# One kernel, five engines: all instruction orders and the PSUM banks of a Mamba-style layer written anew

## The chip, the cores and the metric

The kernel runs on one NeuronCore of a Trainium2 chip. The core has five engines with instruction streams of their own: TensorE (PE, matrix products), VectorE (DVE), ScalarE (ACT, which also evaluates tables of functions), GpSimd (POOL) and SyncE (SP), which here issues every DMA. They meet only at semaphores. The metric is the device time of one launch in microseconds; smaller is better.

## The reference

The input x is 8 x 1024 tokens of 256 channels, float32. All weights are float32 too. What is computed, cut to its core:

```python
# L0_attn, on u = layernorm(x); x = x + result
zxbcdt = u @ W_in.T                      # z0, x0 (512 each), xBC (512+16+16), dt (8 heads)
dt  = softplus(dt + dt_bias);  A = -exp(A_log)
xBC = silu(causal_conv4(xBC) + conv_b)   # depthwise, 4 taps
def step(h, x_t, B_t, C_t, dt_t):        # state 8 heads x 64 x 16, over 1024 tokens
    h   = exp(dt_t * A) * h + dt_t * x_t * B_t
    y_t = h @ C_t + D_param * x_t
y = layernorm(y) * ln_gamma + ln_beta
y = sigmoid(y @ W_gate.T + b_gate) * y
out = concat([silu(z0) * x0, y]) @ W_out.T
# L0_ffn, on layernorm(x); x = x + result
h = gelu(x @ absmean(W_fc))              # absmean: weights rounded to -1, 0, 1
h = layernorm(h) * ln_w + ln_b
out = h @ absmean(W_proj)
```

## The kernel before

**Tiling.** The 8192 tokens are 16 blocks of 512 (two blocks are one sequence), each of 4 chunks of 128 tokens, and the scan works on sub-chunks of 64. A float32 product is made of three float16 products of high and low halves (`products`, line 413), a product with ternary weights of two. Activations are turned by DMA transposes (`xnT`, `yhl`, `x3T`, `hT`) or on TensorE with an identity.

**Steps.** Each engine has a dictionary STEPS from a letter to a small function, and one string that says in which order its steps are issued: PE_ORDER, ACT_ORDER, DVE_ORDER, POOL_ORDER, SP_ORDER (lines 32 to 160). A word is a letter and a block number in hex; on PE the digits behind it are the PSUM banks (0 to 7) that the step writes. The n-th word with the same letter and block is part n of that step. The order of the words is the order of the instructions, and nothing else sets it. Several blocks are in flight at once: between the first convolution of a block and its last projection lie some 350 us, five blocks' worth.

**PE steps**, roughly in the order of one block: `c` convolution inputs (128x512 x6, line 413, and the small one of B and C at lines 483 to 485), `u` and `m` to `q` the decays (`q` line 581), `x` turns x (line 519), `g` the Gram product of B and C (line 555, it reads the tile `crep`), `e`, `b`, `s` small ones, `t` chunk states (line 568), `r` the part of y carried by the states (line 594), `w` the chunk's own part (line 613), `y` turns y (line 622), `G` gate (128x512 x12), `z` and `v` the skip branch (128x512 x6 each), `o` the output product (`wout`, 24 of 128x256), `f` the FFN's first product (line 673, 128x512 x4, two per chunk), `p` its second (line 685, 128x256 x16). `X`, `B`, `O`, `C`, `R` happen once, at the start.

**Waits.** Before a step writes a bank, `take` waits until the engine that last read it is done; other waits are for the operands. Each engine waits in its own order, so a step that waits holds up all that stands behind it. On DVE, `4` (function dt_last, lines 1112 to 1121) is a chain of six small instructions, each of which waits for the one before; `S` moves the state on eight times, `E` multiplies exponentials by the masked Gram matrix (line 1199), `v` (line 1236) and `c` (line 1081) read banks that PE then reuses. On POOL, `l` and `k` make the low halves of `cat` and `caty` (lines 1395, 1391), `n` adds the halves of y (line 1386), `q` and `V` are powers (line 1309). On ACT, exp and ln are in one table set, gelu in another, silu in a third; tanh is in the last two. `load` (line 183) issues ACT_TABLE_LOAD when the function wanted is not in the set that is there, so the order of ACT's steps sets how many loads there are. `E` on ACT (line 853) is the exponential, `F` (line 734) the sum of absolute weights, `g` gelu (line 914), `t` tanh.

**SP** issues DMAs in its order: `h` (xnT, line 1471, high half then low half, and then the load of x), `d` writes C to memory (line 1480), `c` spreads it over the partitions as `crep` (line 1487), `n` turns y (line 1515), `j` turns h (line 1525), `X`, `6`, `r`, `p` the others. A DMA whose data isn't ready holds up all behind it.

```python
def spread_c(i, n):
    sp.wait_ge(ce, i)
    sp.wait_ge(g_mm, i)
    sp.wait_ge(c_out, 32 * (i + 1))
    eng.dma_start(crep[:, :], c_rows[i % 2].unsqueeze(0).broadcast_to([8, 16, T])).then_inc(rep, 16)
```

Of the kernel before, what the change touches and what calls it, by code (L numbers as in the profile page):

```python
# [22 lines left out]
for _n, _w in (("alog", 8), ("dcol", 4), ("lng", 4), ("lnb", 4), ("bg", 4), ("cw", 20), ("cb", 5),  # L23
# [9 lines left out]
    "X00 X01 c02 c03 z04 c05 c06 u07 c00 B01 v02 z03 c17 m05 x01 s06 c10 x04 g035 x01 u14 c17 b06 x00 c13 e05 c14 "  # L33
    "q010 t026 v05 O07 q031 r00263 v01 z04 s15 m17 w0 w0 w0 w0 c24 y00 c27 x12 y06 y03 y01 z05 u24 x10 v02 z16 "
    "g104 c23 x10 z14 b15 e17 v11 x10 c22 c26 q175 G00 G03 t102 C01 G03 G06 r14302 q175 s27 m25 w1 v17 w1 w1 w1 "
    "x26 c31 c35 g247 x23 y10 o02 y11 x24 o07 y10 c36 u33 y11 z12 b23 o07 z10 C04 e21 o05 c34 x21 v17 R03 c31 G15 "
    "v16 G13 q220 z24 t275 q216 G13 G12 f00 r21576 w2 f03 f02 w2 w2 m30 f03 w2 f00 c42 s31 x35 f03 y27 x36 y20 "
    "o15 y24 c42 v27 z26 u43 x35 f07 f00 o11 v22 y27 g335 c44 b30 o11 e33 o15 x30 v27 c43 z21 p00 z26 c42 G25 "
    "q341 G23 t376 G25 v22 G20 z33 q325 p00 f16 v37 r33412 w3 f15 m46 w3 w3 f16 w3 f10 f15 c53 x47 s46 f14 y31 "
    "y30 p02 p07 c55 x43 z32 y31 o27 x44 g430 f16 u55 e41 o23 f10 b46 y37 c55 v34 o20 x43 o26 c57 c51 z30 p13 v32 "  # L40
    "z34 G36 q450 t472 G33 G34 v36 s53 q427 p15 m50 z41 G33 f22 r47654 w4 f23 w4 w4 f20 w4 f22 f23 c60 f27 y46 "
    "x55 v44 y42 p13 p17 y45 c61 u60 z46 x53 g572 o34 f23 x56 y40 c67 e52 f25 b56 o33 v41 o32 x54 o30 c66 p23 c65 "
    "z42 v44 t510 m67 z43 G46 G42 v40 q514 s63 G46 G45 q521 p24 f30 r53214 w5 z56 f37 w5 v55 w5 f36 w5 f30 f35 "
    "c77 x63 f32 y56 p21 y54 p20 c73 y55 x62 z51 o46 u77 e60 c72 x64 y55 o43 g617 b60 f34 v51 f37 o46 x65 o43 c70 "
    "c74 z51 p37 z56 v55 t632 G50 G51 q672 m73 z60 v56 s75 G54 G51 q606 p34 f41 v64 r67320 w6 f46 w6 w6 f41 w6 "
    "f44 f46 x71 c87 y63 p32 f44 y60 p36 x74 c81 y67 z62 e75 u86 o53 x74 y66 v60 b71 f45 g742 o57 c84 o52 f43 x71 "
    "c86 o57 z65 p40 c82 z63 v61 G67 t746 G65 m80 q727 v61 q734 s86 G65 p42 G67 r73461 f55 w7 f50 w7 z72 w7 f57 "
    "w7 f55 c90 f53 x87 y74 p46 f55 y71 c93 p47 y75 v70 z72 x84 e86 u97 o61 x80 b84 o62 y77 g853 f50 c96 v75 o63 "
    "f57 x81 o64 c92 z73 p51 c95 t807 z74 G76 v73 G74 m90 v77 q821 G76 q834 s95 p52 G71 z83 r84560 f67 w8 f62 w8 "
    "w8 f61 w8 f67 f62 ca4 x91 p55 y87 f66 ca0 y82 y86 p51 x97 z84 ua5 o71 b97 v85 e93 f62 x90 g964 o75 y83 v86 "  # L50
    "ca4 f60 o71 ca7 x92 o75 ca3 z81 p60 t962 G85 z84 v87 sa1 G85 ma2 q960 G87 q945 v81 p66 G83 f70 r94516 w9 f77 "
    "w9 w9 f73 w9 f72 f70 cb7 p64 xa3 y95 f71 y92 z96 p60 cb1 v97 y95 ub4 xa3 z96 cb0 ba2 f73 xa7 ea6 y95 o84 o81 "
    "v96 f77 xa4 o85 o82 ga31 cb6 z97 p75 cb3 ta14 G92 G90 mb7 z96 v92 qa14 G95 v90 qa62 p71 G94 f83 ra6201 wa "
    "f85 sb7 wa wa f84 wa p73 f85 f86 cc4 ya2 za0 f85 ya1 xb6 eb7 p73 cc4 ya2 va6 xb5 za3 uc0 o91 xb5 bb0 f82 o93 "
# [1545 lines left out]
```

## Time and profile before

| | |
|---|---|
| median of 3 runs | 1121.73 us (1119.06 to 1123.7) |
| the profiled execution | 1125.57 us |
| its span, first to last instruction | 1123.8 us |
| busy: PE, DVE, ACT, POOL | 1041.4, 981.4, 901.2, 500.2 us |
| mean granted clock of TensorE | 0.973 of full speed |
| ACT_TABLE_LOAD | 129, 165.5 us |

The busy time of PE is a union of overlapping matmuls whose ends are modelled, so the distance between starts says more than the length of one. A row of a timeline merges equal instructions that follow each other. Two of TensorE's clock levels are seen, 1.2 GHz (0.5 of the granted clock) and 2.4 GHz (1.0).

### The profile page before, as it was taken

What the parts mean: (1) busy time and instruction counts of PE and PEld (TensorE: products, weight loads), DVE (VectorE), ACT (ScalarE), POOL (GpSimd) and SP (SyncE); (2) the same over time, 40 slices, a digit from 0 to 9 for tenths busy, and PEclk for the clock granted to TensorE, in tenths of its full rate; (3) what the DMA queues carried; (4) which work ended last, traced back from release to release, by engine and by line L of the source; (5) the groups of instructions that cost most, each with busy time, mean ns of one, the idle gap of its engine ahead of it and who ended that gap; (6) DMA issues with size and microseconds to landing.
All of it is one profiled execution on the core that took longest, in us unless ns stands there. A gap on an engine that the chain in (4) does not pass through costs nothing. (4 is left out here: it accounts for less than half of the span.)

```text
span 1123.8 us, 29390 instructions
## 1 busy us (share of the span) xinstructions
PE 1041.4 (93%) x11470; PEld 661.2 (59%) x11470; DVE 981.4 (87%) x1992; ACT 901.2 (80%) x1593; POOL 500.2 (45%) x590
## 2 busy tenths in 40 slices
PE   5678899999999999999789999989999999999996
PEld 3343656565575756657456575755657565666674
DVE  6899999999989898998977999898999989777765
ACT  5768489878789888987767888988989986877875
POOL 2254562535345543452533435444554534554542
PEclk9889899999999999999998999999999999999998
DMA  8324233555553644455443465533544364263656
GB/s 270 73 58 59 67 61 67 88 98 93 97 109 66 132 74 99 95 88 114 91 76 73 87 114 92 104 64 77 116 92 109 64 110 77 58 124 56 125 118 146
DMA packets 303659, 106.20 MB, mean 94 GB/s; under 512 B 271904, under 2 KB 299808, under 8 KB 303520
## 3 DMA queue, kind: packets, MB, share of 16 engines
q1 hardware_dynamic: 303520, 104.31, 48.1%
q8 instruction: 91, 1.49, 0.5%
q14 instruction: 48, 0.39, 0.1%
HBM read 28.38 MB, written 8.91 MB: 33 GB/s over the span
## 5 line engine op out<-in xcount | busy, mean ns | idle before, releaser
L413 PE MATMUL bank<-xnT,win 128*128 128x512 f16 x1152 | 281.5, 389 | 4.1 <-DVE x L1242 1.9
L413 PEld LDWEIGHTS bank<-xnT,win 128*128 128x128 f16 x1152 | 111.6, 100 | 123.7 <-issue 11.5
L413 PE MATMUL bank<-yhl,wg 128*128 128x512 f16 x768 | 177.1, 383 | 7.7 <-DMA yhl<-ynh 3.0
L183 ACT ACT_TABLE_LOAD x129 | 165.5, 1283 | 2.3
L1395 POOL TENSOR_TENSOR cat<-sz,cat 128x512 f16<-128x512 f32 x64 | 84.0, 1313 | 176.8 <-ACT cat L902 176.7
L1391 POOL TENSOR_TENSOR caty<-tg,caty 128x512 f16<-128x512 f32 x64 | 88.3, 1384 | 132.2 <-ACT caty L890 132.2
L1081 DVE SCALAR_TENSOR_TENSOR cv<-bank,cws,cv 128x511 f32<-128x511 f32 (+2 forms) x192 | 142.8, 746 | 4.5
L685 PE MATMUL bank<-wpj,hT 128*128 128x256 f16 x1024 | 124.0, 276 | 7.4 <-DMA hT<-hb 7.2
L413 PEld LDWEIGHTS bank<-yhl,wg 128*128 128x128 f16 x768 | 73.5, 98 | 97.1 <-issue 9.5
L673 PE MATMUL bank<-wfc,x3T 128*128 128x512 f16 x512 | 129.4, 383 | 0.1
L685 PEld LDWEIGHTS bank<-wpj,hT 128*128 128x128 f16 x1024 | 99.7, 99 | 29.3 <-issue 10.7
L1309 POOL TENSOR_TENSOR rsy<-rsy,mhalf 128x1 f32<-128x1 f32 x64 | 43.6, 681 | 144.2 <-DVE rsy L1218 144.2
L914 ACT ACTIVATE h<-bank,rs 128x512 f32<-128x512 f32 x128 | 87.0, 681 | 25.0 <-PE bank L673 22.0
L413 PE MATMUL bank<-wout,cat 128*128 128x256 f16 x768 | 96.9, 277 | 1.8 <-POOL caty L1391 0.9
L413 PE MATMUL bank<-wout,caty 128*128 128x256 f16 x768 | 95.7, 275 | 0.0
L1256 DVE SCALAR_TENSOR_TENSOR h<-h,hmu,lnwb 128x1024 f32<-128x1024 f32 x64 | 89.5, 1398 | 6.1 <-ACT hsq L930 6.1
L1386 POOL TENSOR_TENSOR yT<-yhl 128x512 f32<-128x512 f16 x64 | 79.1, 1247 | 26.3 <-DMA yhl<-ynh 26.3
L1278 DVE TENSOR_TENSOR hb<-h,hb 128x1024 f16<-128x1024 f32 x64 | 82.3, 1286 | 7.6 <-ACT hb L947 6.0
L413 PEld LDWEIGHTS bank<-wout,cat 128*128 128x128 f16 x768 | 75.6, 99 | 18.0 <-ACT h L914 1.3
L863 ACT ACTIVATE tg<-bank,nmy,rsy 128x512 f32<-128x512 f32 x64 | 49.5, 774 | 40.6 <-POOL nmy L1381 32.9
L413 PEld LDWEIGHTS bank<-wout,caty 128*128 128x128 f16 x768 | 75.9, 99 | 9.4
L947 ACT ACTIVATE hb<-h 128x1024 f16<-128x1024 f32 x64 | 67.2, 1049 | 14.4 <-DVE h L1256 13.5
(167 smaller groups left out, 2099.4 us busy)
## 6 DMA issues: line engine op xcount, KB each, us to landing
x<-in_x SPq DMA_DIRECT2D x31, 512.0 KB, 4.8
out_y<-x SPq DMA_DIRECT2D x15, 512.0 KB, 3.3
crep<-c_rows SPq DMA_DIRECT2D x16, 256.0 KB
hT<-hb SPq DMA_TRANSPOSE x128, 3.2
caty<-in_wg SPq DMA_DIRECT2D x1, 1024.0 KB, 7.3
x<-in_wout SPq DMA_DIRECT2D x1, 1024.0 KB, 9.7
hT<-in_wfc SPq DMA_DIRECT2D x1, 1024.0 KB, 11.7
hb<-in_wpj SPq DMA_DIRECT2D x1, 1024.0 KB, 13.6
```

Of the source, the lines that this page charges most:

```text
L183: self.eng.preload_act_table_set(self.table)
L413: m = eng.matmul(b, lhs(p, k), rhs(q, k), start=(n == 0), stop=(n == len(seq) - 1))
L673: m = eng.matmul(b[:, :], x3T[:, p, c, k, :], wfc[:, k, half * T:(half + 1) * T], start=(k == 0 and p == 0), stop=(k == 1 and p == 1))
L685: m = eng.matmul(b[:, 0:DM], hT[:, buf, p, k, :], wpj[:, k, :], start=(k == 0 and p == 0), stop=(k == 7 and p == 1))
L914: eng.activation(h[:, at % 3, half * T:(half + 1) * T], b[:, :], ACT.Gelu, scale=rs3[:, c:c + 1], accum_out=hsum[:, c, half:half + 1]).the ...
L947: eng.activation(halves[h_halves(i, c)][:, 0, :], h[:, at % 3, :], ACT.Copy).then_inc(hn_hi, 1)
L1081: op = eng.scalar_tensor_tensor(cs[:, j, 3 - k:T], b[:, 0:T - 3 + k], cws[:, j, k:k + 1], cs[:, j, 3 - k:T], ALU.mult, ALU.add)
L1256: eng.scalar_tensor_tensor(h[:, at % 3, :], h[:, at % 3, :], hmu[:, c:c + 1], lnwb[:, :], ALU.subtract, ALU.mult).then_inc(hn, 1)
L1278: eng.tensor_tensor(hh[:, 1, :], h[:, at % 3, :], hh[:, 0, :], ALU.subtract).then_inc(hn_lo, 1)
L1386: eng.tensor_tensor(yf[:, j, :].rearrange("p (c t) -> p c t", c=NCH), yhl[:, :, 0, j, :], yhl[:, :, 1, j, :], ALU.add).then_inc(y_sum, 1)
L1391: eng.tensor_tensor(caty[:, 1, g, :], tg[:, g % 2, :], caty[:, 0, g, :], ALU.subtract).then_inc(yg_lo, 1)
L1395: eng.tensor_tensor(cat[:, 1, j, :], sz[:, j % 2, :], cat[:, 0, j, :], ALU.subtract).then_inc(cat_lo, 1)
```

## The change

The change writes all five order strings anew. No step is added or taken away and no function is altered; the numbers behind PE's words (the banks) are new too. The diff's shape, with one line of each table of before and of after:

```diff
 PE_ORDER = (
-    "X00 X01 c02 c03 z04 c05 c06 u07 c00 B01 v02 z03 c17 m05 x01 s06 c10 x04 g035 x01 u14 c17 b06 x00 c13 e05 c14 "
+    "X00 X01 c02 c03 u04 c05 B06 c07 c00 z01 m02 z04 c13 s05 c17 b00 x02 c11 x05 v03 g024 x07 u13 e00 x03 c15 c12 "
...
 ACT_ORDER = (
-    "W0 a0 a0 h0 h0 W0 c0 N0 c0 c0 a1 h1 10 c0 30 b0 c0 s0 s0 40 c1 z0 z0 50 c1 F0 f0 c1 a2 e0 11 c1 h2 b1 31 l0 "
+    "a0 W0 a0 h0 N0 h0 W0 c0 c0 10 c0 a1 h1 30 c0 s0 c0 F0 b0 40 50 z0 s0 c1 c1 f0 z0 e0 O0 11 c1 a2 h2 31 c1 E0 "
...
 SP_ORDER = (
-    "K0 h0 W0 W0 W0 W0 K0 h1 h1 d0 c0 60 d1 h2 h2 c1 W0 n0 n0 61 n0 n0 h3 d2 c2 h3 r0 n1 n1 n1 n1 62 h4 X0 d3 X0 "
+    "K0 W0 K0 W0 h0 W0 h1 h1 d0 c0 W0 60 h2 h2 d1 c1 61 n0 n0 n0 n0 h3 h3 d2 c2 r0 W0 62 n1 n1 n1 n1 X0 X0 d3 h4 "
...
```

DVE_ORDER and POOL_ORDER are rewritten in the same way. Since `load` follows ACT's order, the number of ACT_TABLE_LOAD changes with it: 129 before, 156 now.

**SP, the loads of `crep`.** The order before, from the transposes of xnT for block 10 to past the `crep` of block 9, with `yhl` the turned y of block 8 and `hT` the turned h of older blocks:

```order
L1471 DMA_TRANSPOSE xnT<-hb 128x8x128 x2
L1426 DMA x<-in_x 128x4x256
L1525 DMA_TRANSPOSE hT<-hb 128x8x128 x3
L1531 DMA out_y<-x2 128x4x256
L1515 DMA_TRANSPOSE yhl<-ynh 128x8x128
L1487 DMA crep<-c_rows 128x1x512
L1499 DMA x2<-in_x 128x4x256
```

The same place in the new order:

```order
L1471 DMA_TRANSPOSE xnT<-hb 128x8x128
L1487 DMA crep<-c_rows 128x1x512
L1471 DMA_TRANSPOSE xnT<-hb 128x8x128
L1426 DMA x<-in_x 128x4x256
L1525 DMA_TRANSPOSE hT<-hb 128x8x128 x3
L1531 DMA out_y<-x2 128x4x256
```

`crep` has moved from behind the first `yhl` to between the two `xnT`; so it has for the blocks before and behind.

**PE, the Gram product of block 9.** What PE has to do before `g` of block 9 (L555), in the order before, from the second turn of y of block 8:

```order
L622 MATMUL bank<-const,yT 128x128 x8
L685 MATMUL bank<-wpj,hT 128x256 x16
L519 MATMUL bank<-const,cv 128x128 x4
L413 MATMUL bank<-xnT,win 128x512 x6
L500 MATMUL bank<-const,bc 128x128 x2
L413 MATMUL bank<-wout,cat 128x256 x12
L413 MATMUL bank<-wout,caty 128x256 x12
L544 MATMUL bank<-const,bcs 128x128 x2
L413 MATMUL bank<-xnT,win 128x512 x6
L527 MATMUL bank<-segL,pick 128x128 x4
L673 MATMUL bank<-wfc,x3T 128x512 x4
L519 MATMUL bank<-const,cv 128x128 x4
L555 MATMUL bank<-crep,bcs 64x64 x8
```

The new order, from the last turn of y of the same block:

```order
L622 MATMUL bank<-const,yT 128x128 x4
L413 MATMUL bank<-wout,cat 128x256 x12
L413 MATMUL bank<-wout,caty 128x256 x12
L544 MATMUL bank<-const,bcs 128x128 x2
L413 MATMUL bank<-wout,cat 128x256 x12
L413 MATMUL bank<-wout,caty 128x256 x12
L413 MATMUL bank<-xnT,win 128x512 x6
L673 MATMUL bank<-wfc,x3T 128x512 x4
L519 MATMUL bank<-const,cv 128x128 x4
L413 MATMUL bank<-xnT,win 128x512 x6
L413 MATMUL bank<-wout,cat 128x256 x12
L413 MATMUL bank<-wout,caty 128x256 x12
L555 MATMUL bank<-crep,bcs 64x64 x8
```

Three output products stand ahead of the Gram product instead of one, and two more halves of the skip branch.

**ACT, the gelus of block 4 and what stands between them** (from the second tanh of the gate, before):

```order
L884 ACTIVATE tg<-bank,bgh 128x512
L812 ACTIVATE cv<-cv 128x1024
L947 ACTIVATE hb<-h 128x1024
L183 ACT_TABLE_LOAD
L914 ACTIVATE h,hsum<-bank,rs 128x512 x2
L890 ACTIVATE caty<-tg 128x512
```

And now, with a load more that a silu between the gelus brings:

```order
L914 ACTIVATE h,hsum<-bank,rs 128x512
L922 ACTIVATE hjunk,hmu<-hsum 128x2
L183 ACT_TABLE_LOAD
L897 ACTIVATE sz<-bank 128x512
L776 ACTIVATE bc<-bank,small,cws 128x256
L890 ACTIVATE caty<-tg 128x512
L183 ACT_TABLE_LOAD
L914 ACTIVATE h,hsum<-bank,rs 128x512
```

A silu (L897) now stands among the gelus of a block, with a load on either side. Counted over the whole order, loads ahead of a gelu rise from 36 to 49 and loads ahead of a silu of the skip branch from 27 to 36.

## Rows read from the trace of the kernel before

**Rows 1.** The page: span, busy time, granted clock of PE in 40 slices
```profile
span 1123.8 us, 29390 instructions
PE 1041.4 (93%) x11470; PEld 661.2 (59%) x11470; DVE 981.4 (87%) x1992; ACT 901.2 (80%) x1593; POOL 500.2 (45%) x590
PEclk9889899999999999999998999999999999999998
```

**Rows 2.** Windows: from:to, length, busy us per engine, PEclk, DMA share, GB/s
```profile
0.00:140.00 140.00, 104.06 (x1189) 62.61 (x1190) 122.09 (x273) 92.03 (x148) 56.61 (x86) 0.89 0.42 105
140.00:350.00 210.00, 201.72 (x2259) 127.56 (x2257) 193.92 (x402) 177.66 (x317) 94.55 (x111) 0.99 0.48 86
350.00:700.00 350.00, 333.90 (x3837) 211.54 (x3838) 314.70 (x639) 288.70 (x510) 152.32 (x185) 0.98 0.50 93
700.00:1050.00 350.00, 338.18 (x3781) 217.87 (x3777) 303.03 (x606) 293.74 (x521) 161.21 (x178) 1.00 0.48 91
1050.00:1123.80 73.80, 63.54 (x423) 41.63 (x421) 47.66 (x76) 49.07 (x101) 35.52 (x31) 0.94 0.61 123
```

**Rows 3.** PE timeline at two Gram products: start, length, ..., idle before, releaser
```profile
518.01 0.48 PE L555 MATMUL bank<-crep,bcs 16*64 16x64 f32 x16 [1.07 <-DMA crep<-c_rows]
...
590.21 0.72 PE L555 MATMUL bank<-crep,bcs 16*64 16x64 f32 x16 [2.89 <-DMA crep<-c_rows]
```

**Rows 4.** SP timeline from the xnT transposes to crep of block 9
```profile
555.48 1.32 SPq L1471 DMA_TRANSPOSE xnT<-hb  x1
...
582.72 1.29 SPq L1515 DMA_TRANSPOSE yhl<-ynh  x1
584.14 0.68 SPq L1487 DMA_DIRECT2D crep<-c_rows  x1
```

**Rows 5.** Windows: two stretches at low clock
```profile
282.30:285.70 3.40, 3.24 (x68) 2.07 (x69) 3.33 (x13) 0.63 (x1) 0.00 (x0) 0.51 0.60 114
...
589.50:596.30 6.80, 6.09 (x42) 4.57 (x43) 4.89 (x12) 5.83 (x11) 2.51 (x3) 0.50 0.57 114
```

**Rows 6.** Timelines of DVE, POOL and PE before the states of block 4
```profile
275.92 1.11 DVE L1120 CAST ahl<-dtt 128x96 f16<-128x96 f32 x1
...
275.81 1.16 POOL L1395 TENSOR_TENSOR cat<-sz,cat 128x512 f16<-128x512 f32 x1
...
282.46 1.96 PE L568 MATMUL bank<-Xd,th 64*32 64x128 f32 x64 [3.86 <-DVE sz L1236]
```

**Rows 7.** Groups: line, op, xcount, busy us, mean ns, idle before; min/median/max ns of two
```profile
L1199 DVE SCALAR_TENSOR_TENSOR EM<-EM,Gm 128x512 f32<-128x512 f32 x64 | 57.7, 943 | 4.4 <-ACT EM L853 4.4
...
L1120 DVE CAST ahl<-dtt 128x96 f16<-128x96 f32 x16 | 8.0, 501 | 0.8 <-DVE dtt L1116 0.3
...
L183 ACT ACT_TABLE_LOAD x129 | 165.5, 1283 | 2.3
...
L1199 DVE SCALAR_TENSOR_TENSOR EM<-EM,Gm x64: 676/684/1651, 63.1 to 1020.0; 128x512 f32<-128x512 f32 x64
...
L1116 DVE TENSOR_SCALAR dtt<-dtt x16: 180/182/1233, 33.1 to 935.9; 128x32 f32<-128x32 f32 x16
```

**Rows 8.** Timelines of ACT and PE at the first states
```profile
50.73 1.28 ACT L183 ACT_TABLE_LOAD   x1
52.02 0.42 ACT L806 ACTIVATE bcs<-bc 128x256 f32<-128x256 f32 x1
...
56.53 0.35 PE L420 MATMUL bank<-gam,hsq 128*128 128x2 f32 x2 [4.07 <-ACT h L734]
58.76 1.54 PE L594 MATMUL bank<-ec,S 32*64 32x64 f32 x81 [1.11 <-ACT EM L853]
```

**Rows 9.** PE timeline at the end
```profile
1079.96 1.47 PE L413 MATMUL bank<-wout,cat 128*128 128x256 f16 x12 [0.86 <-POOL caty L1391]
...
1082.58 1.48 PE L413 MATMUL bank<-wout,cat 128*128 128x256 f16 x12
...
1109.70 1.91 PE L685 MATMUL bank<-wpj,hT 128*128 128x256 f16 x16 [2.48 <-DMA hT<-hb]
```

228 rows, old and new, of tables (ACT_ORDER, DVE_ORDER, PE_ORDER, POOL_ORDER) are left out of this document.

## The prediction

> **What bounds the kernel now.** I read the page's first part first, then a table of windows, then the waits of PE, and only then single places. PE is busy 93% of the span, DVE 87%, ACT 80%, POOL 45% [rows 1]. No order changes that work, so the question is what PE loses and to whom. By windows [rows 2], PE idles 140 - 104.1 = 36 us in the first 140 us, 8.3 us up to 350, 16.1 up to 700, 11.8 up to 1050 and 10.3 in the last 74. That is 82 us idle. A part of the busy time is lost as well, where the granted clock is at its lower level, 1.2 GHz. By the windows' mean levels of 0.89, 0.99, 0.98 and 1.00 that is 15, 2, 7 and 0 us up to 1050. The stretches come behind an idle PE: 3.86 us ahead of the one at 282 [rows 6], 2.89 us ahead of the one at 589 [rows 3]. In the one at 589.5 PE is busy 6.09 of 6.8 us at 0.50, which is the work of 3.0 us at full clock [rows 5].
>
> Who makes PE wait? In the first 140 us DVE is the fuller engine: 122 us busy against PE's 104, and up to 350 it is busy 194 of 210 [rows 2]. DVE fills late, because blocks must pass through taps, states and exponentials before PE has its whole choice of work. Later the waits are single ones, and the late one is a DVE step that should have freed a bank, or a DMA.
>
> DVE itself loses time to POOL. The shape that takes 684 ns in the median (EM, line 1199) takes up to 1651 ns, and 943 in the mean; a tiny TENSOR_SCALAR of dt_last takes 182 ns in the median and 1233 at worst [rows 7]. At 275.92 the CAST of that chain takes 1.11 us, and at 275.81 POOL began an instruction of 1.16 us; both end at 277 [rows 6]. So a DVE instruction with POOL in front of it ends when POOL's ends. The excess over the median on line 1199 alone is 64 x 0.26 = 17 us; the CAST, as small as the TENSOR_SCALAR, has a mean of 501 ns. PE pays for it where DVE is the late one: at 282.46 it had idled 3.86 us for a DVE step that stood behind this chain.
>
> The Trainium skill (SBUF — State Buffer, section Practical consequences) says that a VectorE instruction with two SBUF inputs contends with a GpSimd instruction that reads SBUF, and that whoever issues first holds the pair for the whole instruction while the other fully blocks. The trace agrees [rows 6, 7].
>
> **The change part by part.** All sums stand against the profiled execution, 1125.57 us, of which 1123.8 are the span [rows 1]; it is 3.8 us over the median of the runs, and I take those off at the end.
>
> *The loads of crep.* SP issued crep of block 9 at 584.14, right behind a transpose of y (582.72) that waits for y of block 8; the Gram product waited for it until 590.21 with 2.89 us idle, and the one of block 8 until 518.01 with 1.07 [rows 3, 4]. In the new order crep stands between the two transposes of xnT, which ran about 28 us earlier (the second at 555.48), and nothing that it needs is younger than that. At the same time the Gram product of block 9 has moved back. One output product of 24 matmuls takes 1082.58 - 1079.96 = 2.62 us [rows 9], 0.109 us for 256 columns, so 1.3 us for six matmuls of 512. Two more output products, two more skip halves and one more FFN product (0.9) stand between: some 9 us more cover. The two idles go (3.96 us), and with the second the low clock behind it (3.1 us of 6.09 busy). That is 7 us off; I take 5, since PE then reaches the next DVE wait sooner. Bounds 1 and 7. Nothing is added to PE; of SP's queue, one DMA of 0.68 us [rows 4] now goes ahead of the low half of xnT; the block's convolutions stand several steps further on, so I count nothing, and 0.7 us a block where that cover is missing.
>
> *The start.* PE waited 4.07 us for the second sum of absolute weights on ACT and 1.11 for an exponential that stood behind it [rows 8]. Now ACT does both exponentials ahead of that sum and PE asks for the sum some 4 us of work later, while ACT's sum has also moved later. The one wait stays, the other goes. But DVE is the fuller engine there and its order up to y of block 1 holds the same steps. I take 1 us off, bounds 3 more and 3 less.
>
> *The end.* PE waited 0.86 us for POOL ahead of the last block's output products [rows 9]; ACT now makes the last `caty` half one step behind the last tanh of the gate instead of four. The four output products stand in one piece, so the last FFN begins one projection (16 matmuls of 256 columns, 1.75 us) sooner before the end. What follows is a chain of gelu, square, halves and transposes, on which PE waits 2.48 us ahead of the second projection [rows 9]; it is as long as before and begins sooner. I take 2 us off, bounds 0 and 2.6.
>
> *Everything else on DVE and POOL.* The trace of before can't show which instructions of the new order will meet a POOL instruction. The nearest rows say what is to be had: 17 us on line 1199, and all of DVE's small chains [rows 7]; at most the 8.3 + 16.1 us that PE idles from 140 to 700 and the clock lost there could go. At the worst the collisions fall on more critical steps. I take 4.5 us off, which is near the wait at 282.46 with its clock (3.86 + 1.6): one such place of several. Bounds 12 less and 6 more. The gates also stand further behind their last turned y, and the output products behind the skip branch; I count that as cover, not as gain.
>
> *The table loads.* 27 more at 1283 ns [rows 7] are 34.6 us on ACT, which goes from 901 to 936 us of 1124 and still idles 188. Where ACT has slack a load costs nothing. The cover is its idle time: it is busy 288.7 and 293.7 of 350 us in two windows [rows 2]; with 8 loads (11 us) more in each some 50 and 46 us are left. A load ahead of a gelu or a silu delays the bank that PE wants next. I take 3 us on the path, bounds 0 and 17 (half of them on it).
>
> A rule that speaks against this edit is in the Trainium skill (ScalarE: Activation LUTs, What ACT_TABLE_LOAD costs): a switch costs 1283 ns of load and about 1380 ns of drain. By it the estimate would be 27 x 2.66 = 72 us on ACT. The trace shows the 1283 ns exactly and no drain behind it: the load at 50.73 ends at 52.01, and the activation behind it starts at 52.02 [rows 8]. The sum doesn't use the drain.
>
> Sum: 5 + 1 + 2 + 4.5 - 3 = 9.5 us off, 1116.1 for the profiled execution and **1112 us** for the median.
>
> **The rivals.** *The collisions go for the most part.* If the new order keeps POOL out of DVE's way while DVE leads, up to 350 us, the 12 us come instead of 4.5, two more of the low-clock stretches go (3 us), and the loads cost nothing (3): 1112.2 - 7.5 - 3 - 3 = 1099. For it: DVE leads for a third of the run. Against: POOL's work is the same 500 us, so it must run at some time.
>
> *New waits for old ones.* PE's work is the same, DVE's is the same, and the same few steps of DVE (states, exponentials, y) still end ahead of the same PE steps. Then the crep gain is eaten by the next DVE wait, and another PE step meets a late bank. Only the tail stays: 1121.7 - 2, within 2.5 us either way: 1120.
>
> *ACT becomes the late one.* Place: gelus and silus of one block, which now alternate. A load between two gelus holds the bank of the FFN's first product 1.28 us longer and all behind it, the tanh of the gate too. Where PE waits for L914 or L884, half of the 27 loads come on the path (17 us) and two low-clock stretches with them (5): 1121.7 + 22 - 8 = 1136. It decides from the point where ACT's idle in a 350 us window falls under some 30 us. Against: 50 and 46 us are left.
>
> *The change doesn't do what it says*: a static order that fits its planner's durations and not the chip's. It would look like the second or the third rival; it has no price of its own.
>
> **How the numbers follow.** My forecast 0.32, collisions gone 0.20, new waits 0.27, ACT late 0.21. A measurement can tell about 0.5%, or 5.6 us. Faster by more than that is below 1116.1: the forecast's near side (0.30) and the collisions (0.20), 0.50. Within 0.5%: new waits and a little of the forecast, 0.28. Slower: 0.22. The range holds 1094 (the collisions gone, and 5 lower) to 1134, leaving out a tenth at each end, with the unknown costs in it; the likeliest case alone would be 1103 to 1118.
>
> **What would show it.** Of the crep step: no idle on line 555 at blocks 8 and 9, and a full clock behind it. Of the start: PE idle in the first 140 us within 3 us of 36. Of the end: no wait on POOL ahead of the last output products. Of the collisions: the mean of line 1199 under 943 ns. Of the loads: 156 at 1283 ns, and PE's waits for ACT hardly longer. I am wrong if PE's idle from 140 to 1050 is over 36 us, or if the clock lost there is over 9.

## The result, and the profile after

The changed kernel takes **1075.11 us** (median of 4 runs, 1074.0 to 1075.92); the kernel before, measured beside it, 1122.45 (4 runs, 1119.06 to 1123.7). The ratio is 0.958, its 95% interval 0.956 to 0.961: 47 us faster. The prediction said 1112 and a range of 1094 to 1134. The direction was right, the size was wrong by 37 us, and the time lies outside the range.

The page of the profiled execution after (its time is 1074.0 us), span, busy times and granted clock, answers to [rows 1]:

```profile
span 1072.2 us, 29421 instructions
PE 1021.1 (95%) x11470; PEld 652.2 (61%) x11470; DVE 935.9 (87%) x1992; ACT 933.3 (87%) x1620; POOL 489.9 (46%) x590
PEclk9989999999999999999999999999999999999999
```

The same windows as in [rows 2], the last one shorter (columns: from:to, length, busy us of PE, PEld, DVE, ACT and POOL with their instructions, PEclk, DMA share, GB/s):

```profile
0.00:140.00 140.00, 106.07 (x1263) 65.52 (x1264) 121.94 (x296) 99.68 (x161) 58.17 (x91) 0.96 0.40 110
140.00:350.00 210.00, 208.48 (x2527) 130.36 (x2526) 192.15 (x407) 191.79 (x340) 100.49 (x117) 1.00 0.50 94
350.00:700.00 350.00, 346.60 (x3825) 224.06 (x3825) 320.54 (x694) 320.14 (x560) 161.82 (x195) 1.00 0.52 98
700.00:1050.00 350.00, 345.55 (x3753) 222.02 (x3751) 289.28 (x581) 310.68 (x541) 164.71 (x185) 1.00 0.51 94
1050.00:1072.20 22.20, 14.39 (x111) 10.26 (x108) 11.98 (x17) 11.04 (x22) 4.70 (x6) 1.00 0.83 166
```

Span less busy time of PE is 82.4 us before and 51.1 after: 31 us less idle. PE's busy time fell by 20.3 us with the same 11470 matmuls. That part is clock: the mean granted clock is 0.973 of full speed before and 0.994 after, so 30 and 7 us of the spans were lost at the lower level. Less idle and less busy time together are the 51.6 us between the spans (a part of the lost clock falls on idle time). Idle went from 36 to 34 us in the first 140 us, from 8.3 to 1.5 up to 350, from 16.1 to 3.4 up to 700, from 11.8 to 4.5 up to 1050.

DVE's and POOL's busy time fell too, by 45 and 10 us, with the same instructions. This is the place that the prediction underrated. The small chain of dt_last (lines 1112 to 1121, six operations that hand each other their result) in the kernel before, for block 5, DVE and then POOL (start, length, then the operation):

```profile
272.32 0.18 DVE L1112 SCALAR_TENSOR_TENSOR dtv<-u,dtt 128x32 f32<-128x32 f32 x1
272.54 1.13 DVE L1113 TENSOR_TENSOR dtv<-dtv,dtt 128x32 f32<-128x32 f32 x1
273.71 1.08 DVE L1115 TENSOR_TENSOR dtt<-dtv,aneg 128x32 f32<-128x32 f32 x1
274.82 1.07 DVE L1116 TENSOR_SCALAR dtt<-dtt 128x32 f32<-128x32 f32 x1
...
277.07 1.28 DVE L1121 TENSOR_TENSOR ahl<-dtt,ahl 128x96 f16<-128x96 f32 x1
...
272.47 1.16 POOL L1395 TENSOR_TENSOR cat<-sz,cat 128x512 f16<-128x512 f32 x1 [8.20 <-ACT cat L902]
273.58 2.27 POOL L1386 TENSOR_TENSOR yT<-yhl 128x512 f32<-128x512 f16 x2
```

and the same chain of the same block after:

```profile
262.12 0.18 DVE L1112 SCALAR_TENSOR_TENSOR dtv<-u,dtt 128x32 f32<-128x32 f32 x1
262.34 0.19 DVE L1113 TENSOR_TENSOR dtv<-dtv,dtt 128x32 f32<-128x32 f32 x1
262.57 0.19 DVE L1115 TENSOR_TENSOR dtt<-dtv,aneg 128x32 f32<-128x32 f32 x1
262.79 0.18 DVE L1116 TENSOR_SCALAR dtt<-dtt 128x32 f32<-128x32 f32 x1
...
263.26 0.26 DVE L1121 TENSOR_TENSOR ahl<-dtt,ahl 128x96 f16<-128x96 f32 x1
...
263.44 1.16 POOL L1395 TENSOR_TENSOR cat<-sz,cat 128x512 f16<-128x512 f32 x1 [1.19 <-ACT cat L902]
```

Before, each of DVE's five later operations ends with one of POOL's; the chain takes 6.0 us. After, POOL begins its wide operation when the chain is all but over, and the chain takes 1.4 us. So it is the engines' order that semaphores alone tie together, not their speed: here POOL slows DVE with no semaphore between the two. From first start to last end, the chains of blocks 1 to 15 sum to 41.1 us before and 21.9 after (both worked out from the trace); ten of them were held by wide operations of POOL before, one after (block 8, 2.4 us).

The groups that answer to [rows 7] (line, operation, count, busy us, mean ns, idle before):

```profile
L1199 DVE SCALAR_TENSOR_TENSOR EM<-EM,Gm 128x512 f32<-128x512 f32 x64 | 51.2, 842 | 0.8 <-ACT EM L853 0.7
...
L1120 DVE CAST ahl<-dtt 128x96 f16<-128x96 f32 x16 | 3.4, 214 | 0.6
...
L183 ACT ACT_TABLE_LOAD x156 | 200.1, 1283 | 2.8
```

L1120 fell from 501 to 214 ns, L1199 from 943 to 842. Over all of DVE, what its instructions took beyond the median of their line (those with over 0.03 us of it) sums to 86.6 us before and 37.9 after. I call this DVE's **held time** below. The six lines of dt_last hold 20 us of it before and 1 after.

**PE's loss by its progress.** Windows of equal time hold different work in the two kernels. So for each run I took the time at which PE had done so many us of its work (994.5 us in all; each step at the duration that it has undisturbed) and took that work off. What is left is idle and lost clock so far, in us:

| work done | before | after | e1 | e2 | e3 | e4 | e13 |
|---|---|---|---|---|---|---|---|
| 50 | 41.2 | 41.2 | 41.5 | 39.6 | 41.3 | 41.3 | 40.9 |
| 100 | 53.5 | 43.3 | 44.2 | 53.0 | 53.6 | 44.0 | 43.3 |
| 200 | 60.1 | 46.3 | 56.2 | 70.3 | 58.7 | 47.4 | 46.8 |
| 475 | 76.6 | 52.2 | 75.5 | 75.1 | 66.7 | 52.0 | 52.8 |
| 550 | 93.4 | 55.2 | 91.2 | 77.9 | 75.7 | 55.0 | 63.4 |
| 700 | 105.7 | 59.5 | 105.6 | 82.8 | 79.2 | 58.9 | 74.4 |
| 900 | 115.7 | 64.1 | 115.2 | 88.3 | 83.3 | 63.1 | 82.8 |
| 990 | 120.5 | 71.0 | 120.0 | 93.2 | 86.9 | 67.9 | 87.7 |

(e1 to e4 and e13 are experiments below.) Of the 49.5 us between before and after, 10.2 arise between 50 and 100 of work (the trace's 90 to 150 us), 14 by 475, 14 between 475 and 550 (some 530 to 640 us), 8 by 700, 3 behind.

### The profile page after: what moved, and what is told of

It is laid out like the page before. It is cut to its first block, busy times and chain, and to the rows that moved or that the text cites. A ratio compares the mean times of both kernels' runs of the same rounds, so it can differ in the third digit from the quotient of the medians.

```text
span 1072.2 us, 29421 instructions
## 1 busy us (share of the span) xinstructions
PE 1021.1 (95%) x11470; PEld 652.2 (61%) x11470; DVE 935.9 (87%) x1992; ACT 933.3 (87%) x1620; POOL 489.9 (46%) x590
## 4 chain that ended last, share of the span: by engine, by line
PE 69%; DVE 14%; ACT 7%; issue 5%; DMA 3%; SPq 1%; POOL 1%; DVEq 0%; ACTq 0%; POOLq 0%
PE bank L413 41%; PE bank L673 8%; PE bank L685 7%; PE bank L613 3%; PE bank L594 2%; DVE cv L1081 2%; PE bank L622 2%; PE bank L519 2%; DVE sty L1214 1%; ACT L183 1%; DMA x<-in_x 1%; PE bank L568 1%; DVE yT L1206 1%; DVE st L1036 1%; DVE Xd L1143 1%
## 5 line engine op out<-in xcount | busy, mean ns | idle before, releaser
L413 PE MATMUL bank<-xnT,win 128*128 128x512 f16 x1152 | 275.5, 383 | 3.5 <-DVE th L1169 1.2
L1391 POOL TENSOR_TENSOR caty<-tg,caty 128x512 f16<-128x512 f32 x64 | 83.0, 1297 | 189.6 <-ACT caty L890 189.5
L685 PE MATMUL bank<-wpj,hT 128*128 128x256 f16 x1024 | 122.4, 273 | 6.3 <-DMA hT<-hb 5.6
L685 PEld LDWEIGHTS bank<-wpj,hT 128*128 128x128 f16 x1024 | 98.5, 98 | 27.4 <-issue 8.2
L1309 POOL TENSOR_TENSOR rsy<-rsy,mhalf 128x1 f32<-128x1 f32 x64 | 48.0, 750 | 113.8 <-DVE rsy L1218 113.6
L413 PE MATMUL bank<-wout,cat 128*128 128x256 f16 x768 | 94.4, 273 | 0.5 <-DVE th L1169 0.5
L1256 DVE SCALAR_TENSOR_TENSOR h<-h,hmu,lnwb 128x1024 f32<-128x1024 f32 x64 | 87.2, 1362 | 5.2 <-ACT hsq L930 5.2
L413 PEld LDWEIGHTS bank<-wout,caty 128*128 128x128 f16 x768 | 75.1, 98 | 8.7
L673 PEld LDWEIGHTS bank<-wfc,x3T 128*128 128x128 f16 x512 | 46.2, 98 | 45.3 <-issue 2.9
```

Of the source, the lines that this page charges most:

```text
L413: m = eng.matmul(b, lhs(p, k), rhs(q, k), start=(n == 0), stop=(n == len(seq) - 1))
L673: m = eng.matmul(b[:, :], x3T[:, p, c, k, :], wfc[:, k, half * T:(half + 1) * T], start=(k == 0 and p == 0), stop=(k == 1 and p == 1))
L685: m = eng.matmul(b[:, 0:DM], hT[:, buf, p, k, :], wpj[:, k, :], start=(k == 0 and p == 0), stop=(k == 7 and p == 1))
L1256: eng.scalar_tensor_tensor(h[:, at % 3, :], h[:, at % 3, :], hmu[:, c:c + 1], lnwb[:, :], ALU.subtract, ALU.mult).then_inc(hn, 1)
L1391: eng.tensor_tensor(caty[:, 1, g, :], tg[:, g % 2, :], caty[:, 0, g, :], ALU.subtract).then_inc(yg_lo, 1)
```

## The experiments

Times are medians; "against before" is the ratio to the kernel before, run on the same chip beside it, with its 95% interval. In the order strings a word is a step letter, a block (hexadecimal) and, for PE, its banks.

### Is the gain made where it shows? (e1, e2, e13)

The order strings of one kernel up to a point in time, those of the other behind it, on all five engines. The edit, for e1 (e2 with the two kernels' parts exchanged; e13: the cut where the changed kernel is at 600 us):

```
 for each engine:
-    ORDER = order_before
+    ORDER = [w for w in order_after if step(w) in started_by_155us_before]
+          + [w for w in order_before if step(w) not in started_by_155us_before]
```

> The kernel before, with the changed kernel's order for every step that the kernel before starts within its first 155 us, on all five engines, and its own order for the rest. By PE's progress through its work, the changed kernel had 11 to 12 us of its gain of 47 there by that place and the rest behind it. If the gain is made where it shows, this kernel is faster by 9 to 13 us (1110 to 1113 us). If the start only sets up the rest (engines enter block 4 with another lead over PE, and the later gain follows from it), it is faster by over 20 us. If the start's gain is given back at the next place where PE waits for VectorE, by under 4 us.

> The other half: the kernel before's order for every step that it starts within its first 155 us, the changed kernel's order for the rest. If each part of the gain is made where it shows: 35 to 37 us faster than before (1085 to 1088 us). If the start sets up the rest: 10 to 25 us faster. If the start's share is caught up later, 44 us or more.

Measured: e1 1119.6 us, against before 0.997 (0.995 to 1.000); e2 1095.57 us, 0.977 (0.973 to 0.980). Both missed their first numbers, -3 and -26 us for -11 and -36. By its time alone e1 fits its third theory (given back at the next place, under 4 us), though PE's wait there is for ACT and not for VectorE. The table tells where it goes: up to 100 of work e1 has the changed kernel's loss (44.2) and e2 the old one (53.0); at the joint PE then waits once in each, the first matmuls of the segment products (L581):

```profile
151.24 0.64 PE L581 MATMUL bank<-segR,segL 27*64 27x512 f16 x4 [2.92 <-ACT tg L884]
```

```profile
168.15 0.64 PE L581 MATMUL bank<-segR,segL 27*64 27x512 f16 x4 [11.03 <-issue]
```

(e1 above, e2 below; in brackets the idle before, which in e2 ends with nothing that the profile names.) From 100 to 200 of work e1 loses 12.0 us where the kernel before loses 6.6, and e2 17.3 where the changed one loses 3.0: the joints cost 5 and 14 us, the low clock behind the waits included. Behind them, from 200 to 990, e1 loses 63.8 us, as the kernel before does (60.4), and e2 22.9, as the changed one does (24.7). So the start doesn't set up the rest: each stretch has its own price. A joint, though, isn't free, and I had counted none.

> The changed kernel's order for every step that it starts within its first 600 us, the kernel before's order behind it, on all engines. By PE's progress the changed kernel had 38 of its gain there, and 11 come behind. Where the orders were joined at 155 us, the joint itself cost PE 8 and 14 us. If each stretch keeps what it gains: 1084 us and the joint's price, so 1084 to 1098. If what is gained early is lost behind (the old order waits for the same things whenever it comes): over 1108.

Measured: 1091.12 us, 0.973 (0.970 to 0.975). As the first theory has it: the changed kernel's loss up to 475 (52.8 for 52.2), 8 us more at the joint, and from 550 to 990 24.3 us, where the kernel before loses 27.1 and the changed one 15.8. Held time follows the order at once: from 630 to 980 us it is 13.8 us in the changed kernel and 29.7 here.

### Is it POOL's wide operations? (e3, e4, e9, e12)

From block 1 on, the four operations of POOL that take 128x512 elements become a power of 128x4, whose waits and signals are the same; what they computed is left out. The edit of e3, on the kernel before, at one of the four:

```
+            eng.memset(pk[:, :], 0.37)
+            def four(to):
+                return eng.tensor_tensor(to, pk[:, :], mhalf[:, :], ALU.pow)
...
             def rest_cat(i, j):
-                eng.tensor_tensor(cat[:, 1, j, :], sz[:, j % 2, :], cat[:, 0, j, :], ALU.subtract)
+                four(cat[:, 1, j, 0:4])
```

> The kernel before with its order untouched; from block 1 on, GpSimd's four wide operations (the sums of the y halves, the two rests of the gated products, and the bias added to x2) are replaced by a power of 128x4 elements, whose row lasts about as long (1273 ns beside 1247 to 1444) but which moves 4 columns where the wide ones move 512. So the rest halves, the y sum and that bias are left out of the computation. Theory 'collisions': VectorE and GpSimd hold each other up when both stream wide operands (86.6 us on VectorE beyond its lines' medians in the kernel before, 37.9 after), and most of the gain of 47 us is the part of that which stood on the path: here VectorE's excess falls under 20 us and the kernel is faster by 25 to 45 us (1078 to 1097). Theory 'cover': the new order only puts more other work ahead of what waits, and collisions are a by-product: the time falls by under 12 us.

> The changed kernel with the same replacement on GpSimd from block 1 on (the same parts of the computation left out). 'Collisions': little is left to win, 3 to 12 us below the changed kernel (1063 to 1072), and the two quiet kernels stand within 20 us of each other. 'Cover': it falls by as much as the quiet kernel before, and the distance between the two stays 35 us or more.

Measured: e3 1090.53 us, 0.973 (0.969 to 0.976), 31 us faster. e4 1072.61 us, 0.956 (0.952 to 0.960), 2.5 below the changed kernel, which the intervals can't tell from none. The two quiet kernels stand 18 us apart, where the kernels stood 47. The page's busy line of e3 and the same DVE group as above (its line number is 1201 here), and POOL's row for the substitute:

```profile
PE 1030.4 (95%) x11470; PEld 659.0 (61%) x11470; DVE 911.0 (84%) x1992; ACT 899.7 (83%) x1593; POOL 445.2 (41%) x591
...
L1201 DVE SCALAR_TENSOR_TENSOR EM<-EM,Gm 128x512 f32<-128x512 f32 x64 | 45.6, 756 | 7.9 <-ACT EM L855 7.8
...
L1314 POOL TENSOR_TENSOR cat<-pk,mhalf 128x4 f16<-128x4 f32 x60 | 66.7, 1111 | 184.7 <-ACT cat L904 184.2 <-issue 0.4
```

The power takes 1.11 us and holds nobody: DVE's held time is 13.6 us (11.4 of it in the first 140 us, which e3 leaves as they were), in e4 1.5. This is "collisions", and "cover" falls: it had said under 12 us. But 73 us less held time gave 31, and in the changed kernel 36 us less gave 2.5. What a held microsecond costs depends on where it is. One thing e3 changes besides: POOL itself is 55 us less busy (500.2 to 445.2). Whether some of the 31 us comes from POOL being done earlier, e3 can't tell apart; e15 below puts two powers more in 15 blocks of the changed kernel, 33 us of POOL, and they cost 2.

e9 makes the substitution in block 0 and in the preparation of the weights as well.

> The kernel before with GpSimd's wide operations replaced by powers of 128x4 elements in block 0 too, and in the preparation of the gate's and the output's weights (their rests, the z rests, the y sums and the bias are left out everywhere; only block 0's rests of y times gate stay wide). With them quiet from block 1 on it took 1090.5 us, and its start was as slow as before. VectorE has 11.4 us beyond its lines' medians in the first 140 us of the kernel before, 1.0 in the changed one. If collisions make the start slow too: 5 to 11 us below that (1080 to 1086). If the start is slow by its order: within 2.5 us of 1090.5.

Measured: 1088.97 us, 0.972 (0.967 to 0.976), runs from 1083.5 to 1094.3. The median says "within 2.5 us of e3", the spread of the runs is wider than the question, so this one is inconclusive. By PE's progress its profiled run has lost 49.6 us at 100 of work, between e3's 53.6 and e4's 44.0: some 4 of the start's 10 us may be collisions, the rest is order.

e12 makes it for the z rest alone, the line shown in the edit above.

> The kernel before, where from block 1 on one of GpSimd's four wide operations alone, the rest of the gated z, is replaced by a power of 128x4 elements (60 instructions; the low halves of that product are left out of the computation). All four together gave 31 us. The trace before had this operation start against VectorE's chain of small dt steps (the casts held for 1.1 us each). If the gain comes from that chain: 12 to 22 us faster with this one alone. If it is spread over all wide operations by their number (60 of 210): 7 to 10 us. If the collisions only count when all are gone (the next wait takes over): under 5 us.

Measured: 1106.32 us, 0.986 (0.983 to 0.989): 15.5 us, half of e3's gain by 60 of 210 instructions, as the first theory has it. Held time fell by 20.8 us to 65.8, the chains of dt_last from 41.1 to 30.6 us. So it isn't the number of wide operations, it is the ones at the wrong place. The chain accounts for half of the held time that went, 10.5 of 20.8 us; the gain isn't its alone.

### Is it their place in time, or their work? (e17, e14, e15)

e17 leaves the kernel before all its work and its order, and adds 10 waits to POOL:

```
+            def stand_aside(i, n):
+                pool.wait_ge(a_hl, i + 1)
...
-    "... a6 B1 y3 l3 n3 n3 l3 ..."
+    "... a6 B1 y3 g5 l3 n3 n3 l3 ..."
```

(a_hl is counted up by the last operation of dt_last; g is the new step, here ahead of the first z rest of block 3, beside dt_last of block 5.)

> The kernel before with all its work and its order, and 10 added waits on GpSimd: in each of 10 blocks, the first of its wide operations that in the trace before ran beside VectorE's dt_last (six small operations: 3.4 us on average there, 1.4 where nothing ran beside) now waits until dt_last has ended. If the placing in time is what counts: dt_last falls to 1.4 to 1.9 us a block, 15 to 19 us less on VectorE, and the kernel is faster by 6 to 16 us (1106 to 1116). If only less work on GpSimd's side helps, or if GpSimd's own delay costs as much: within 3 us of before, or slower.

Measured: 1108.27 us, 0.988 (0.985 to 0.992): 13.4 us faster. POOL's row after the new wait (its idle before counts from the last thing it did), and the groups of the chain's fifth and second operations (mean ns behind the busy us):

```profile
270.62 1.16 POOL L1398 TENSOR_TENSOR cat<-sz,cat 128x512 f16<-128x512 f32 x1 [9.54 <-DVE ahl L1121]
```

```profile
L1120 DVE CAST ahl<-dtt 128x96 f16<-128x96 f32 x16 | 3.4, 213 | 0.8 <-DVE dtt L1116 0.3
...
L1113 DVE TENSOR_TENSOR dtv<-dtv,dtt 128x32 f32<-128x32 f32 x16 | 3.1, 192 | 0.6
```

The chains sum to 21.1 us, no more than after the change. dt_last's own held time fell by 20 us to nothing, some 4 us more came up on other lines (held time in all is 71 us), and the time fell by 13.4 (9.5 to 17). That is two thirds of what the chain won. What POOL's delay costs is in that; PE's waits for crep grew from 4.0 to 6.4 us here.

e14 goes the other way, in the changed kernel: POOL waits for the logarithm that releases dt_last and then runs two wide operations. e15, its control, runs two powers.

```
+            def beside_dt(i, n):
+                pool.wait_ge(dt_ln, i + 1)
+                for _ in range(2):
e14:                 then(eng.tensor_tensor(spare, ones16 ..., ones16 ..., ALU.add))
e15:                 then(eng.tensor_tensor(spare[:, 0, 0:4], pk, mhalf, ALU.pow))
...
-    "... c3 n1 n1 V0 k1 c3 ..."
+    "... c3 n1 n1 V0 g3 k1 c3 ..."
```

> The changed kernel, with two added wide operations on GpSimd (128x512, both operands from one constant tile, the result unused) in each of blocks 1 to 15 that start when VectorE's last dt step (dt_last, six small operations) may start. If collisions there cost what they seemed to in the kernel before (1.0 to 1.1 us for each held operation, one or two a block): dt_last grows from 1.4 to 2.4 to 3.5 us a block, and the kernel is slower by 12 to 30 us than the control. If the chain has cover: by under 4 us.

> The control: the same waits at the same places of GpSimd's order, with two powers of 128x4 elements in place of the two wide operations; each lasts about as long (some 1.1 us) and moves little. If the price is in the wide operands: within 3 us of the changed kernel (1075 to 1078), and dt_last stays at 1.4 us. If it is GpSimd's time and its waits that cost: as slow as with the wide ones.

Measured on one chip: e14 1091.94 us, 0.974 (0.972 to 0.975); e15 1077.18 us, 0.961 (0.959 to 0.963). The wide operations cost 14.8 us over powers of the same length, the waits and the powers 2. The chain of block 2 in e14, DVE and then POOL (line numbers of DVE are up by 2 in both):

```profile
104.35 1.08 DVE L1115 TENSOR_TENSOR dtv<-dtv,dtt 128x32 f32<-128x32 f32 x1
105.46 0.19 DVE L1117 TENSOR_TENSOR dtt<-dtv,aneg 128x32 f32<-128x32 f32 x1
105.69 1.02 DVE L1118 TENSOR_SCALAR dtt<-dtt 128x32 f32<-128x32 f32 x1
...
103.23 2.15 POOL L1317 TENSOR_TENSOR spare<-ones 128x512 f16<-128x512 f16 x2
105.46 1.21 POOL L1407 TENSOR_TENSOR cat<-sz,cat 128x512 f16<-128x512 f32 x1
```

and in e15 the POOL operations at the same place, and one of DVE beside them:

```profile
101.84 2.17 POOL L1317 TENSOR_TENSOR spare<-pk,mhalf 128x4 f16<-128x4 f32 x2
...
102.94 0.19 DVE L1115 TENSOR_TENSOR dtv<-dtv,dtt 128x32 f32<-128x32 f32 x1
```

The chains sum to 43.0 us in e14 and 20.9 in e15; held time is 65.7 and 37.3 us. So 22 us more on the chain, and 28 us more of held time in all, cost 15: two thirds of the chain's length again. In e14 the added pair also pushes POOL's next wide operation (105.46) onto the rest of the chain, as the old order did.

### The transfers of crep and SP's order (e5, e6, e18)

```
-    "... X5 j4 d8 X5 j4 j4 h9 h9 j4 j4 j5 p4 n7 c8 r6 ..."
+    "... X5 j4 d8 X5 j4 j4 h9 c8 h9 j4 j4 j5 p4 n7 r6 ..."
```

(e5; so for blocks 8 to 15. c is the load of crep, h a transfer of xnT.)

> The kernel before with one edit: SyncE's loads of crep for blocks 8 to 15 stand between the next block's two xnT transfers, as in the changed kernel, instead of behind them and their neighbours. In the trace before, PE waited 4.0 us for crep at two places (blocks 8 and 9), with 3.4 us more at half clock behind the second. If the term of the prediction holds: 3 to 7 us faster (1114 to 1119), and PE waits for crep no more. Rival: the engines behind it wait for something else by then, under 1.5 us.

Measured: 1117.26 us, 0.996 (0.994 to 0.999), 4 us faster with an interval of 2 to 6. PE's waits for crep went from 4.0 us to one of 1.1 ("no more" was expected). The size of the term holds. That it is the crep wait alone isn't shown: in the profiled run, the fastest of its ten (1110.5 us), dt_last's chains are shorter too, 36.8 us for 41.1.

e6 is the changed kernel with the whole SP_ORDER string of the kernel before.

> The changed kernel with SyncE's order of the kernel before (the order of the transfers; the other four engines as changed). If the order of the transfers carries a part of the gain by itself: slower than the changed kernel by 3 to 7 us (1078 to 1082), with PE waiting for crep around blocks 8 and 9. If the other engines' new lead covers it: within 2 us of 1075.

Measured: 1114.74 us, 0.995 (0.994 to 0.996). Neither theory: 40 us slower than the changed kernel. Of PE's waits in it those that grew most (waited for, us in total, times, longest):

```profile
PE bank L685 <- DMA hT<-hb: 13.4, 6, 4.6
...
PE bank L483 <- DMA xnT<-hb: 9.2, 3, 8.4
PE bank L622 <- DVE yT L1206: 5.3, 3, 2.8
...
PE bank L555 <- DMA crep<-c_rows: 3.8, 2, 3.0
```

In the changed kernel L685 waits 5.6 us for hT, and PE for no transfer of xnT or crep. One wait of 8.4 us here is for an xnT transfer that stands too late in SP's queue. Held time is 36.3 us, as low as in the changed kernel. So avoided collisions are no gain by themselves: the transfers' order has to be the one that the other four orders were laid for. It doesn't say that SP's order would bring 40 us in the kernel before; there its one part that could be moved alone brought 4.

e18 joins e5's edit to that of e17.

> The kernel before with two edits together: GpSimd's 10 waits beside dt_last, and SyncE's crep loads of blocks 8 to 15 between the xnT transfers. Alone they gave 13.4 and 4 us. With the first alone PE waited 6.4 us for crep, against 4.0 before. If the gains add: 16 to 19 us faster (1103 to 1106). If the crep wait is the one that took over: 19 to 25 us (1097 to 1103). If a third wait takes over both: 13 to 15 us (1107 to 1109).

Measured: 1106.0 us, 0.987 (0.983 to 0.990): 16 us by the medians, the sum of the two within their intervals. The interval, 11 to 19 us, also holds the third theory (13 to 15) and e17's 13.4 alone. Waits for crep fell from 6.4 us (e17) to 2.6:

```profile
  PE bank L555: 2.6, 1
```

### The table loads (e7, e10, e11)

> The kernel before with 27 redundant loads of ScalarE's table (the load ahead of the gelu of 27 places is made twice): 156 loads of 1283 ns, as many as the changed kernel has, 34.6 us more on ScalarE. The prediction's term was +3 us (0 to 17). If ScalarE's slack covers them: 0 to 6 us slower (1121 to 1128). If ScalarE is as late as the others at these places: 10 to 17 us slower.

Measured: 1122.83 us, 1.001 (1.000 to 1.003), and it measures nothing: two loads of one table back to back leave one in the profile, L183 stands at x129 as before. So e10 and e11 load another table first and use it:

```
             last, self.table = self.table, SETS.get(func, "silu_and_others")
+            if self.table == "gelu_and_others" and first <= n <= first + 26:
+                detour = "Exp" if last == "silu_and_others" else "Silu"
+                self.eng.preload_act_table_set(SETS[detour])
+                eng.activation(spare[:, n:n + 1], none[:, 0:1], getattr(ACT, detour))
             self.eng.preload_act_table_set(self.table)
```

> The kernel before with 27 detours on ScalarE: ahead of 27 of its 36 loads of the gelu's table it loads another table and runs one activation of 128x1 elements under it. That is 156 loads, as many as the changed kernel has, and 27 small activations; some 35 us of loads and a few of activations more on ScalarE. The prediction's term for 27 loads was +3 us (0 to 17). If ScalarE's idle time covers them: 0 to 5 us slower than before (1122 to 1127). If they stand on the path: 10 to 30 us slower.

> The changed kernel with the same 27 detours (ahead of its 12th to 38th load of the gelu's table): 183 loads. If its order still leaves ScalarE idle where they fall: 0 to 6 us slower than the changed kernel (1075 to 1081). If the gain stands on ScalarE being on time at these places, with the slack spent: 10 to 35 us slower (1085 to 1110). The more it loses against the kernel before with the detours, the more the loads' price is one of the order's own lead, not of a load.

Measured: e10 1129.94 us, 1.008 (1.005 to 1.011), 8 us slower (median of 8 runs; the profiled one, 1140.49 us, is the slowest); e11 1098.2 us, 0.979 (0.977 to 0.981), 23 us slower than the changed kernel. The added rows, alike in both:

```profile
L187 ACT ACT_TABLE_LOAD x27 | 34.6, 1283 | 0.5
...
L709 ACT ACTIVATE spare<-none 128x1 f32<-128x1 f16 x27 | 5.5, 203 | 0.3
```

The same 40 us on ScalarE cost 8 where it idles 223 us and 23 where it idles 139. That fits a changed order that lives on ScalarE's slack; but the detours also stand at other places in the two orders, and the runs don't separate the two.

### Is there more at the start? (e16)

```
-    "... x14 u20 y03 e16 y01 v02 g170 ..."
+    "... x14 y03 e16 y01 v02 u20 g170 ..."
```

> The changed kernel with one step of PE's order, the transposes of block 2's dt columns (u, for which PE waits 5.0 us at 69.8 us, with 6.8 us at half clock behind), moved behind the next four steps (y, the C half of e, y, the last v of block 0). If these four are ready before it: 1 to 5 us faster than the changed kernel (1070 to 1074). If they wait for the same late VectorE, or if the dt chain behind u then ends last: within 1 us, or slower.

Measured: 1077.21 us, 0.961 (0.959 to 0.963), no better than the changed kernel's 0.958 (0.956 to 0.961). In the changed kernel PE waits 4.96 us for line 1078 of DVE ahead of this step, at 75.4 us; here it waits 3.49 us for the same line at 75.6, ahead of the step that took its place, and 1.7 us more at 84. What is late is the DVE work, not the step. No version here beats the changed kernel.

## Why the prediction was wrong in size and right in sign

**Everything else on DVE and POOL (4.5 us off, bounds 12 off and 6 on): this is the step that failed.** The mechanism was right and was seen in the rows; its size was not summed. e3 puts it at 31 us in the kernel before and e4 at 2.5 in the changed one, so at some 28 for the change, where the sum had 4.5; e17 gets 13.4 with ten waits, e14 gives 15 back. Three things went wrong. First, I priced one place, the wait at 282.46, "one such place of several", and didn't count them. The view by groups gave the count: the mean less the undisturbed duration, over the six lines of dt_last, is some 1.25 us a block, 20 us in all, beside the 17 on line 1199 that I did write down. Second, the upper bound of 12 was drawn from what PE idles between 140 and 700 us. That window alone held 24 us of idle and 9 of lost clock, and the gain of e3 ran on to 990 of work. Third, held time has no one price. On the chain of six small operations it is two thirds (e17: 20 us shorter, 13.4 gained; e14: 22 longer, 15 lost). On the other lines it is near nothing in the changed kernel (e4: 36 us less held, 2.5 gained). In the kernel before they can't be so cheap: of e3's 73 us less held 19 are the chains, which at two thirds make 12 of the 31 us gained, and an estimate of 19 us is left for the other 54. I had put all into one guess.

**The clock** wasn't a term of its own. It carries 20 us of the 51.6 between the profiled spans. It looks like no cause of its own: PE's low stretches stand behind its waits, in the joint of e2 as in [rows 5], and in e3, where no order differs, none of the four between 140 and 1050 us is at its place (282, 559, 589, 934) and one came new at 617. But it also varies between runs of one kernel (last section). My check "wrong if the clock lost from 140 to 1050 is over 9" holds with some 2.

**crep (5 off, 1 to 7): right in size.** e5 gives 4 (2 to 6), in the old order; in the changed kernel L555 waits for crep nowhere. What I took at nothing, the other transfers that are moved with it, e6 shows to be needed as a whole.

**The start (1 off, within 3): wrong**, 10 us by PE's progress. My check on it, PE idle in the first 140 us within 3 of 36, came true (33.9) and told nothing: the gain there is clock (0.89 to 0.96 in the window) and work done earlier. At most 4 of the 10 are collisions (e9, inconclusive); the rest is open.

**The end (2 off, 0 to 2.6): right in kind.** No wait for POOL stands ahead of the last output products; from 950 of work to the end of the span the loss is 3.6 us smaller (9.9 for 13.5), clock included. But just ahead, from 900 to 950, the changed kernel loses 3.6 us more, with a wait of 1.55 us that ends at 966.4 and a low clock at 968. The chain at the end is as long as I said: PE's longest wait there is 2.87 us for hT (2.48 before).

**The table loads (3 on, 0 to 17):** not shown in the changed kernel by itself. As a price it is 8 us in the old order, within the bounds. The next 27 in the new cost 23, more than the upper bound, so the point at which ScalarE becomes the late one may be near. "ACT becomes the late one" didn't come: 156 loads, 139 us of ACT's idle left, and PE's waits for ACT 18 us before and 15 after.

**The rivals.** "The collisions go for the most part" was the right one, at a chance of 0.20, and its 1099 was 24 us too slow, since I let it work only up to 350 us. "New waits for old ones" I had held for nearly as likely as the forecast, and the 47 us refute it. e18 alone couldn't: its 16 us fit two gains that add and don't exclude one that was taken over.

**The account, as far as the runs carry it:** collisions behind block 0 some 28 us (e3's 31 less e4's 2.5, POOL's own shorter time included). The quiet kernels are 18 us apart, by PE's progress 9.6 by 100 of work and 9.4 behind. Of the first, up to 4 may be collisions and some 6 the start's order; of the latter crep may be 4. Which of the reordered steps bring the remaining 5, and what the 27 loads took from them, stays open.

## What to carry to other kernels

Sum held time before forecasting: for every line of VectorE and GpSimd the mean less the median, times its count, and then sort it by whether the line is in a chain of small steps that PE waits for (two thirds of it came back here) or is wide (near 0 in the changed order, an estimated third in the old). Where such a chain meets the other engine's wide operations, a wait that lets the chain pass is a cheap first step: ten waits brought 1.2% here, of the 4.2% that five new orders brought. Count a lost clock with the waits ahead of it, and don't judge a stretch by its idle time alone.

## What was unexpected about the chip

- An operation of 0.18 to 0.26 us that meets a wide one takes 1.0 to 1.3 us and ends with it; when it ends, POOL's next wide one has begun, and holds DVE's next. That is how one collision becomes five (6.0 us for 1.4). The Trainium skill (SBUF — State Buffer, section Practical consequences) names tensor_scalar and cast among those that can take the shared ports in their two-port modes; the trace agrees: the TENSOR_SCALAR of 128x32, with one input, takes 1.07 us at 274.82. The CAST of [rows 6], for which the prediction named the rule of two inputs, has one input as well; of the rows it pointed at, line 1199 has two.
- Which operations get held is sharp. I took, from the traces before and after, all of DVE's instructions that start while a 128x512 operation of POOL has 0.2 us or more to go. With two inputs in SBUF 141 of 148 are held; CAST, COPY and TENSOR_SCALAR of 4 or more columns with their input in SBUF, 27 of 29. With an operand in PSUM (`bank`) none of 439 is, with the statistics (BATCH_NORM) none of 147, with TENSOR_SCALAR of one column none of 39. POOL is held in turn: its subtraction of 1.16 us (line 1395, median) takes up to 2.23.
- A power of 128x4 elements keeps POOL busy for 1.11 us and holds nothing (e15: dt_last stays at 1.4 us in all 15 blocks, with two powers released together with it). So length on POOL isn't what hurts. Whether it is the width or the kind of operation isn't shown: no run has a wide power, and POOL's narrow additions last only 0.2 us.
- The time lost at the lower clock varies from run to run: 19 to 30 us over 59 runs of the kernel before, median 26, against 5 to 11 in 4 runs of the changed one, which also lie closer together (2 us, against 5 for the 4 runs of the kernel before beside them).
